# State-space mixer block: short matmuls woven between the steps of the long products, the recurrence over chunks put ahead of the masks, and the states' products copied by ScalarE

## The reference, cut to what matters

```
bc = einsum('bti,oi->bto', value, W_bc).reshape(B, T, H, 4, N)
bc = bc / (sqrt(sum(bc * bc, -1)) + EPS)
Bz, Bx, Cz, Cx = bc[..., 0, :], bc[..., 1, :], bc[..., 2, :], bc[..., 3, :]
def step(carry, inp):                       # one position; z, s: (B, H, N, DH)
    S = 1 / (1 + dt * k + dt * dt * A)
    z = S * (z - dt * A * s + dt * (Bz x u))
    s = s + dt * z + dt * (Bx x u)
    y = Cz . z + Cx . s
```

## Time and profile before

| what | value |
|---|---|
| median of three runs | 2529.51 us (2527.91 to 2533.37) |
| the profiled execution, its own time | 2518.47 us |
| its span, first to last instruction | 2516.8 us |
| mean granted TensorE clock | 0.912 of full speed |
| PE busy | 2091.9 us (83%), 31266 instructions |
| DVE busy | 2073.7 us (82%), 5467 instructions |
| ACT busy | 1055.9 us (42%), 1572 instructions |
| DVE L1066, masks: idle before it | 170.3 us, ended by PE L693 (scores) in 170.1 of them |
| PE L693, scores: idle before it | 95.3 us, of them 94.7 "issue" |
| PE L668, products | 1015.5 us busy, 2048 records of 642 ns on average |

### The profile page before, as it was taken

How to read it: one execution, slowest core, us unless ns; L and a number is a source line. 1 busy time by engine, 2 the same in 40 slices (tenths; PEclk the granted TensorE clock), 3 DMA queues, 4 the chain that set the end, 5 groups by cost and what they waited for, 6 DMA issues and landing times. The chain is left out here.

```text
span 2516.8 us, 78402 instructions
## 1 busy us (share of the span) xinstructions
PE 2091.9 (83%) x31266; PEld 1101.6 (44%) x31266; DVE 2073.7 (82%) x5467; ACT 1055.9 (42%) x1572; POOL 83.5 (3%) x28
## 2 busy tenths in 40 slices
PE   6784498988998998889888988998999899538886
PEld 2332144444444444444444444444444444327775
DVE  6885789988898898889888988898898886567775
ACT  4654244433443444344434444343444433204444
POOL 0000000000000000000000000000000000043310
PEclk9897799999998999999989999999998999668997
DMA  3565555444454454545444554555454334163300
GB/s 129 199 204 167 135 121 118 121 115 112 115 133 111 105 115 116 116 110 129 122 119 108 124 116 103 116 143 115 102 119 114 96 90 106 38 250 136 134 25 26
DMA packets 224669, 300.31 MB, mean 119 GB/s; under 512 B 96784, under 2 KB 114192, under 8 KB 218128
## 3 DMA queue, kind: packets, MB, share of 16 engines
q1 hardware_dynamic: 174416, 212.11, 33.2%
q10 hardware_dynamic: 48704, 78.68, 11.5%
q0 software_dynamic: 1152, 4.19, 0.5%
HBM read 240.85 MB, written 50.86 MB: 116 GB/s over the span
## 5 line engine op out<-in xcount | busy, mean ns | idle before, releaser
L668 PE MATMUL m_ps_a<-m_valT,m_w_bc 128*128 128x512 f32 x2048 | 1015.5, 642 | 61.1 <-DMA m_valT<-scratch_valT 33.4
L668 PEld LDWEIGHTS m_ps_a<-m_valT,m_w_bc 128*128 128x128 f32 x2048 | 397.5, 205 | 607.6 <-issue 602.7
L804 ACT ACTIVATE m_sq<-m_ps_a 128x512 f32<-128x512 f32 x256 | 152.9, 597 | 862.1 <-PE m_ps_a L668 817.5
L926 DVE TENSOR_TENSOR m_prod<-m_psi,m_shear 128x128 f32<-128x128 f32 x960 | 367.9, 383 | 1.1 <-ACT m_shear L794 1.0
L930 DVE TENSOR_TENSOR m_psi<-m_psi,m_prod 128x128 f32<-128x128 f32 x960 | 367.6, 383 | 0.5 <-issue 0.5
L680 PE MATMUL m_ps_s<-m_sq,m_head_sum 128*32 128x512 f32 x512 | 267.9, 606 | 24.4 <-ACT m_sq L804 24.4
L1066 DVE TENSOR_TENSOR m_g<-m_ps_g,m_causal 128x512 f32<-128x512 f32 x128 | 87.5, 687 | 170.3 <-PE m_ps_g L693 170.1
L693 PE MATMUL m_ps_g<-m_q,m_k 32*64 32x64 f32 x8192 | 129.3, 240 | 95.3 <-issue 94.7
L805 ACT ACTIVATE m_raw<-m_ps_a 128x512 f32<-128x512 f32 x256 | 151.6, 592 | 0.0
L693 PEld LDWEIGHTS m_ps_g<-m_q,m_k 32*64 32x64 f32 x8192 | 112.3, 140 | 89.2 <-issue 87.4
L221 PE MATMUL ps_w<-p_xnT,w_in 128*128 128x512 f32 x256 | 117.8, 613 | 17.4 <-ACT gate L284 17.2
(11 more groups left out here) (142 smaller groups left out, 3028.9 us busy)
## 6 DMA issues: line engine op xcount, KB each, us to landing
m_scale<-scratch_norm SPq DMA_DIRECT2D x256, 256.0 KB, 5.0
m_w_bc<-in_w_bcT ACTq DMA_DIRECT2D x252, 256.0 KB, 3.4
m_shear<-scratch_n_alpha SPq DMA_DIRECT2D x64, 256.0 KB, 5.1
m_shear<-scratch_beta SPq DMA_DIRECT2D x256, 64.0 KB, 3.8
m_det<-scratch_gd SPq DMA_DIRECT2D x256, 64.0 KB, 4.1
scratch_gateT<-gate SPq DMA_DIRECT2D x8, 1024.0 KB, 3.9
scratch_valT<-val SPq DMA_DIRECT2D x8, 1024.0 KB, 4.4
scratch_svgT<-svg SPq DMA_DIRECT2D x8, 1024.0 KB, 6.1
```

The costliest lines, as they stand in the source:

```text
L668: mm = pe.matmul(ps_a[j % 2].ap(), w_bc[:, j, kt, :], valT[:, kt, :], start=(kt == 0), stop=(kt == KI - 1))
L804: act.activation(sq[:, j % 2, :], ps_a[j % 2].ap(), ACT.Square).then_inc(sq_ready.sem, sq_ready.step)
L926: dve.tensor_tensor(prod.ap(), psi_t[half][:, :, :, :, t], shear_t[half][:, :, :, t].unsqueeze(1).to_broadcast([P, 2, 2, HALF * NC]), ALU. ...
```

## The change

In words, by engine:

- **TensorE.** `products` becomes `product(b, group, j, parts)`, which issues some of a product's four matmuls. `inner` and `outputs` now hold them between their short matmuls: product 0 is cut in three (two matmuls ahead of the states' products, one among them, one behind), product 1 in four between pairs of the scores, product 2 stays whole and stands behind the scores, product 3 is cut in four within `outputs`. Each `sum_squares` moves with its products; the last one (j = 3) moves behind `outputs`. No matmul is added or taken away.
- **ScalarE.** A new `copy_dX` copies the states' products out of `ps_g` into SBUF (`dX`), two instructions a unit, behind `store_y`. Evacuations 1 and 2, `scale_beta` and `det_inverse` move to the end of the unit before.
- **VectorE.** The recurrence over the chunks stands ahead of the two masks and reads `dX` from SBUF. Two of the `advance(1)` are dropped, and the masks have none.
- TensorE waits for `dX_ready` before the scores, since they overwrite the banks in which the states' products stand.

The core of the diff:

```
+                def product(b, group, j, parts):
+
+                    for kt in parts:
+                        if kt == 0:
+                            pe.wait_ge(w_in[j].sem, w_in[j].at(b, group))
+                            pe.wait_ge(raw_ready.sem, raw_ready.at(b, group * NJ + j - 2))
+                        if group % HG == 0 and j == 0:
+                            pe.wait_ge(val_in[kt].sem, val_in[kt].at(b, group // HG))
+                        mm = pe.matmul(ps_a[j % 2].ap(), w_bc[:, j, kt, :], valT[:, kt, :],
+                                       start=(kt == 0), stop=(kt == KI - 1), skip_group_check=True)
+                        if kt == KI - 1:
+                            mm.then_inc(a_made.sem, a_made.step)
+                        elif group % HG == LAST and j == NJ - 1:
+                            mm.then_inc(val_used[kt].sem, val_used[kt].step)
...
-                def inner(b, group):
+                def inner(b, group, ahead):
 
                     s = group % 2
+                    if ahead:
+                        product(b, group + 2, 0, (0, 1))
                     pe.wait_ge(kT_ready.sem, kT_ready.at(b, group * 2 + 1))
                     pe.wait_ge(u_in[s].sem, u_in[s].at(b, group // 2))
                     pe.sem_inc(passed, 1)
-                    chunk_states(s).then_inc(dX_made.sem, dX_made.step)
+                    for c in range(NC - 1):
+                        if ahead and c == NC // 2:
+                            product(b, group + 2, 0, (2,))
+                        chunk_states(s, c)
+                    if ahead:
+                        product(b, group + 2, 0, (3,))
+                    pe.wait_ge(dX_ready.sem, dX_ready.at(b, group))
                     pe.wait_ge(q_ready.sem, q_ready.at(b, group))
-                    scores(s)
+                    for c in range(NC):
+                        scores(s, c)
+                        if ahead and c % 2:
+                            product(b, group + 2, 1, (c // 2,))
+                    if ahead:
+                        sum_squares(b, group + 2, 0)
+                        product(b, group + 2, 2, range(KI))
+                        sum_squares(b, group + 2, 1)
...
                     inner_outputs(s, 0).then_inc(even_outputs.sem, even_outputs.step)
                     if more:
-                        sum_squares(b, group + 2, NJ - 1)
+                        product(b, group + 2, 3, (0,))
                     pe.wait_ge(X_ready.sem, X_ready.at(b, (group + 1) * (NC - 1) - 1))
                     pe.sem_inc(passed, 1)
                     for c in range(1, NC):
-                        cols = slice(c * C, (c + 1) * C)
-                        for part in range(2):
-                            for h in range(HP):
-                                heads = slice(h * N, (h + 1) * N)
-                                mm = pe.matmul(ps_y[h * N:h * N + DH, cols], X[heads, c - 1, part, :],
-                                               q[s][heads, part, cols], start=False, stop=(part == 1),
-                                               skip_group_check=True)
+                        outer_outputs(s, c)
+                        if more and c in (2, 4, 6):
+                            product(b, group + 2, 3, (c // 2,))
+                    if more:
+                        sum_squares(b, group + 2, 2)
                     pe.wait_ge(even_outputs.sem, even_outputs.at(b, group))
                     pe.sem_inc(passed, 1)
                     inner_outputs(s, 1).then_inc(y_made.sem, y_made.step)
+                    if more:
+                        sum_squares(b, group + 2, 3)
...
+                def copy_dX(b, group):
+                    act.wait_ge(dX_made.sem, dX_made.at(b, group))
+                    act.wait_ge(X_ready.sem, X_ready.at(b, group * (NC - 1) - 1))
+                    for odd in range(2):
+                        count = NC // 2 - odd
+                        ins = act.activation(dX[:, odd:NC - 1:2].rearrange("p c r d -> p c (r d)"),
+                                             ps_g[:, 2 + odd, PAIRS * C:PAIRS * C + count * 2 * DH
+                                                  ].rearrange("p (c e) -> p c e", c=count), ACT.Copy)
+                    ins.then_inc(dX_ready.sem, dX_ready.step)
...
-                            evacuate(b, group + 2, 1, loads)
-                            evacuate(b, group + 2, 2, loads)
-                        if not last:
-                            scale_beta(b + 1, group)
-                        if here:
-                            det_inverse(b, unit)
-                        if more:
-                            evacuate(b, group + 2, 3, loads)
+                            evacuate(b, group + 2, 3, not (last and group == LAST - 2))
                             norms(b, group + 2)
                         if here:
                             copy_kT(b, unit)
                         store_y(b, group)
-                        if not (last and group >= LAST - 2):
+                        if here:
+                            copy_dX(b, unit)
+                        if ahead:
                             evacuate(b, group + 3, 0, not (last and group == LAST - 3))
                         if more:
                             det_log(b, group + 2)
+                        if not last and group == 0:
+                            scale_beta(b + 1, 0)
+                        if not last and group < LAST:
+                            scale_beta(b + 1, group + 1)
+                        if ahead:
+                            evacuate(b, group + 3, 1, not (last and group == LAST - 3))
+                            evacuate(b, group + 3, 2, not (last and group == LAST - 3))
+                        if more:
+                            det_inverse(b, group + 2)
...
-                        for two in range(2):
...
-                        dve.wait_ge(dX_made.sem, dX_made.at(b, group))
+                        dve.wait_ge(dX_ready.sem, dX_ready.at(b, group))
                         dve.wait_ge(coef_ready.sem, coef_ready.at(b, group))
                         dve.wait_ge(y_made.sem, y_made.at(b, group - 1))
                         for c in range(NC - 1):
                             if c:
-                                dve.tensor_tensor(V.ap(), ps_dX(c), X[:, c - 1], ALU.add).then_inc(own.sem, own.one())
+                                dve.tensor_tensor(V.ap(), dX[:, c], X[:, c - 1], ALU.add).then_inc(own.sem, own.one())
                                 v_made = own.n
                                 advance(1)
                                 dve.wait_ge(own.sem, v_made)
-                            into = V.ap() if c else ps_dX(0)
+                            into = V.ap() if c else dX[:, 0]
...
+                        for two in range(2):
+                            heads = slice(two * 2, two * 2 + 2)
+                            dve.wait_ge(g_made.sem, g_made.at(b, group))
```

More of the change, by code:

```diff
@@ L697, in chunk_states, with scores @@
[L697 to L703, removed]
-                                               skip_group_check=True)
-                    return mm
+                def scores(s, c):
+                    cols, into = slice(c * C, (c + 1) * C), slice(c // 2 * C, (c // 2 + 1) * C)
+                    for part in range(2):
+                        for h in range(HP):
+                            heads = slice(h * N, (h + 1) * N)
+                            mm = pe.matmul(ps_g[rows_of(c), h, into], k[s][heads, part, cols], q[s][heads, part, cols],
+                                           start=(part == 0), stop=(part == 1), skip_group_check=True)
+                    if c == NC - 1:
+                        mm.then_inc(g_made.sem, g_made.step)
@@ new lines, in chunk_states @@
+                def chunk_states(s, c):
+                    for part in range(2):
+                        for h in range(HP):
+                            heads = slice(c // 2 * P + h * N, c // 2 * P + (h + 1) * N)
+                            mm = pe.matmul(ps_dX(c)[h * N:(h + 1) * N, part, :], kT[rows_of(c), part, heads],
+                                           u[rows_of(c), s, c // 2, h * DH:(h + 1) * DH], start=True, stop=True,
+                                           skip_group_check=True)
+                    if c == NC - 2:
+                        mm.then_inc(dX_made.sem, dX_made.step)
@@ L735, in inner_outputs, with outer_outputs @@
                     return mm
+                def outer_outputs(s, c):
+                    cols = slice(c * C, (c + 1) * C)
+                    for part in range(2):
+                        for h in range(HP):
+                            heads = slice(h * N, (h + 1) * N)
+                            pe.matmul(ps_y[h * N:h * N + DH, cols], X[heads, c - 1, part, :],
+                                      q[s][heads, part, cols], start=False, stop=(part == 1),
+                                      skip_group_check=True)
```

(6 more changed lines are left out.)

46 lines of the change are left out of this document (18 added, 28 removed).

## The result

The changed kernel takes 2459.23 us (median of four runs, 2456.68 to 2460.15) against 2528.71 for the kernel before in the same session: a ratio of 0.9729, 95% interval 0.9699 to 0.9759. Forecast were 2453 and a range of 2390 to 2530. The profiled execution took 2456.68, its span is 2455.0, its mean granted clock 0.942.

A forecast was written before the change was run, and what follows sets the result against it. TensorE bounds at 27.1 us a unit: eight make 216.8, the loop's branch 223.4, late units 226.4 a row. Seven rows 10.4 shorter plus 3 from the last give 2442.7 profiled, 2453 median; range 2390 to 2530.

The forecast's parts named there:

- The bound: TensorE bounds the changed kernel at 27.1 us a unit, VectorE's and the norms' circles 0.6 to 1.3 us behind.
- Masks and order: On VectorE, masks moved behind the recurrence find the scores done: the 170.1 us wait at L1066 goes, to under 20.
- The issue stops: On TensorE inside the scores: short matmuls outrun instruction fetch; weaving takes 94.7 us of stops to under 15.
- The price of a cut: On TensorE, each of eight cuts in the products costs 0.19 us, 1.5 us a unit; upper bound 0.41.
- Waits on ScalarE: TensorE waits 0.3 us a unit for the keys' copies and 0.3 for the dX copies.
- The norms' circle: From masks through outputs, square roots and gather back to the masks' end: 26.5 us, just inside TensorE's 27.1.
- L966 waiting in most units: Profile sign at VectorE's gathered norms that would show the forecast wrong, in favour of rival D.
- rival D: Norms' circle or the two waits on ACT are longer, 28 us a unit: row 230.6, 2483 us; chance 0.17.
- The sum: Row of eight units 226.4 us instead of 236.8, last row gives 3; profiled execution 2442.7, median 2453.
- A: Rival: TensorE's cuts cost more, one drained edge 0.41 instead of 0.19; row 240.5, 2552 us; chance 0.12.
- B: Rival: TensorE's issue stops stay and only move; row 238.4, 2537 us; chance 0.07.
- The drain rule: On TensorE, changing tiling mode drains the engine, so each cut drains twice; alone it speaks for the upper bound 0.41.

The follow-up runs named there:

- product 3 whole: Changed kernel with product 3 as one whole block behind the even inner outputs, three cuts fewer: 2407.86 us, 0.9577 of the kernel before.
- the fine pair: Changed kernel with sums of squares 2 and 3 as neighbours ahead of the odd inner outputs: 2395.46 us, 0.9489 of the kernel before.
- the unwoven kernel: Changed kernel with TensorE's products 0 to 3 as whole blocks again, all else as changed: 2444.61 us, 0.9671 of the kernel before.

## Why the prediction was right, and where it was off

**The bound.** Right: TensorE bounds the changed kernel. It idles for 9 us a row, 0.95 us a unit less work on it (product 3 whole) came through at 38 to 51 us, and in the fine pair its savings came through in full. VectorE's 162.0 us at the gather are the other side of this: no run shows that they cost this kernel anything by themselves.

**Masks and order.** Right: the masks' wait is gone, and undoing that part alone costs the woven kernel 170 us.

**The issue stops.** Right in cause and size (under 15 forecast, 0.7 found). But the prediction let this pay for the weaving, and in the unwoven kernel, with the dX wait in between, 56 of the 94.7 us went without it. The step left out a side effect of the other part of the change.

**The price of a cut.** Mis-sized: 0.19 predicted, 0.28 measured in the timeline over eight cuts, 0.32 by taking three away. The rows at hand had both edges of a product, but not the restart of a short run, which costs about 0.1. A unit's work is 27.26 and not 26.5.

**Waits on ScalarE.** 0.3 and 0.3 predicted; 0.47 and 0.31 in the unit shown, 43 us over the kernel. Right in place and size.

**The norms' circle.** It was put just inside TensorE's time, and was. But the prediction had also named "L966 waiting in most units" as the sign of rival D, the case of 28 us a unit, and both came: VectorE waits in 60 of 64 units, and a unit took 28.04 us. What made the unit that long was not D's circle or its longer waits, but the price of the cuts. The sign could not tell the two apart, since an engine that does not bound waits somewhere in every unit. The circle itself had slack: the masks still end 1.4 us before TensorE asks (the scan, which follows them, begins at 1319.14, the outputs at 1320.57).

**The sum.** A row was forecast at 226.4; seven rows took 1605.6 us from first to last L1046 (313.96 to 1919.56), 229.4 each, 21 us more in all. Outside the seven rows 10.8 us went, where 3 had been counted. The profiled execution was therefore 14 us above its forecast (2456.7 against 2442.7). The median came within 7 only because the 11 us between profiled execution and median did not recur; they were 2.5 here. So part of the closeness is luck. The measured row is nearer to D's 230.6 than to the forecast's 226.4. The chances also do not add up as told: A and half of B are 0.155 before any room, where 0.14 is given.

**The drain rule.** The Trainium skill (TensorEngine Tiling (Array Packing), Key Properties) says that a change of tiling mode drains the engine; every cut here is such a change twice, and the timelines put it at 0.28 to 0.32 a cut, a fifth to a third under the 0.41 of rival A; no run shows how much of that is the drain. The statement of the Trainium skill (Runtime: NRT & Kernel Launch, Instruction fetch mechanics) that crossing from one 16 KiB block of instructions to the next is mostly hidden does not hold for this stream, if the stops are read as the fetch: they took 94.7 us, kept to fixed places of the stream, and went with the length of the run.

One thing said ahead of the prediction needs mending: the scores do not overwrite the columns in which the states' products stand. They go to other columns of the same PSUM banks; TensorE waits for dX so that it does not write a bank that ScalarE is reading. Leaving that wait out was not tried for that reason, so no run shows what it would do.

## What to carry to other kernels

When a run of hundreds of tiny matmuls stops with the reason "issue", break it once with long work (that alone gave 33 us here); every further cut has a price on both sides of it, here about 0.3 us. Before reordering an engine's work around a wait, see whether the order on the consumer is the real fault: here the consumer's new order and its copies gave 76 us without any weaving, and the fine weaving on top of them nothing. And ask of the last instruction of a chain, here one sum of squares, what starts behind it and what stands beside it: moving it ahead of one block of 32 records gave 52 to 64 us.

## What was not expected of the hardware

Two float32 matmuls of 128x512 with 32 output columns each, into different partitions of one PSUM bank, take 1.02 us as neighbours (1.03 in the median of 62 units) and 0.98 us each when something stands between them. This holds where both inputs are ready: where the second one's was made just ahead, the pair took 1.39. Moving one instruction so that two of them meet is worth nearly the whole second one.
